# Rotary pieces of a latent attention: made at 512 queries at a time, without the second set of products, with the exchanged rows moved by GpSimd

## The reference, cut to what matters

```python
c_q, c_kv = h @ w_down_q.T, h @ w_down_kv.T          # 64 numbers a token each
q = (c_q @ w_up_q.T).reshape(b, s, H, DH)            # 16 heads of 64
k = (c_kv @ w_up_k.T).reshape(b, s, H, DH)
v = (c_kv @ w_up_v.T).reshape(b, s, H, DH)
# rope: of each head, with even rows e and odd rows o
rot = stack([e * cos - o * sin, e * sin + o * cos])
scores = einsum('bhqd,bhkd->bhqk', q, k) / sqrt(64)
out = softmax(scores) @ v
out = out @ w_out.T + x
```

## Time and profile before

| | |
|---|---|
| time of one execution, median of 3 | 2020.72 us (2020.29 to 2023.2) |
| the profiled execution: its own time | 2017.2 us |
| its span in the profile | 2015.4 us |
| PE busy | 1864.9 us (93%) |
| DVE busy | 1583.6 us (79%) |
| ACT busy | 1288.5 us (64%) |
| POOL busy | 1067.1 us (53%) |
| granted TensorE clock, mean | 0.97 |

### The profile page before, as it was taken

One profiled execution on the slowest core, in us unless ns is written; L12 is line 12 of the kernel. 1 busy time (PEld: TensorE's weight loads), 2 busy tenths in 40 slices (PEclk: granted clock), 3 DMA queues, 4 the chain that ended last, 5 costly groups with the idle time before them and its releaser, 6 DMA issues. The chain is left out here.

```text
span 2015.4 us, 36125 instructions
## 1 busy us (share of the span) xinstructions
PE 1864.9 (93%) x11446; PEld 928.7 (46%) x11446; DVE 1583.6 (79%) x2378; ACT 1288.5 (64%) x2678; POOL 1067.1 (53%) x1219
## 2 busy tenths in 40 slices
PE   5767898889868999999999999999999999999798
PEld 2553585458543444443444443444443444444446
DVE  6788865786556888887888887888888888888455
ACT  5555783578336777776777776777776777777321
POOL 0637742674226566565656655665665666566200
PEclk9898999999978999999999999999999999999799
DMA  1100302030065999988998998899899899998353
GB/s 38 66 1 6 82 3 74 6 82 3 14 263 184 331 336 343 328 321 308 324 343 325 340 333 301 318 325 346 324 334 333 310 323 335 338 333 324 127 117 74
DMA packets 201609, 454.24 MB, mean 225 GB/s; under 512 B 12064, under 2 KB 159264, under 8 KB 200256
## 3 DMA queue, kind: packets, MB, share of 16 engines
q1 hardware_dynamic: 201408, 451.76, 63.9%
HBM read 230.86 MB, written 206.83 MB: 217 GB/s over the span
## 5 line engine op out<-in xcount | busy, mean ns | idle before, releaser
L1680 ACT ACTIVATE g.probs<-g_score,g.lowest 128x1024 f32<-128x1024 f32 x514 | 567.9, 1109 | 333.3 <-DVE g.lowest L1666 333.3
L1666 DVE TENSOR_REDUCE g.lowest<-g_score 128x1 f32<-128x1024 f32 x514 | 605.7, 1220 | 186.8 <-PE g_score L1634 186.8
L1634 PE MATMUL g_score<-g.keys,g.queries 64*128 64x512 f32 x2056 | 501.6, 606 | 19.6 <-issue 11.3
L1776 DVE STREAM_TRANSPOSE g.blocks<-g.probs 128x768 f32<-128x768 f32 x512 | 467.3, 952 | 0.9
L1696 PE MATMUL g_mix_ps<-g.far,mid.y_tok 128*64 128x512 f32 x1560 | 378.1, 606 | 0.0
L1634 PEld LDWEIGHTS g_score<-g.keys,g.queries 64*128 64x128 f32 x2056 | 183.9, 188 | 249.5 <-ACT g.probs L1680 130.6
L1736 POOL TENSOR_TENSOR g.scaled<-g.scaled,g.coef 128x1024 f32<-128x1024 f32 x66 | 125.1, 1896 | 236.9 <-ACT g.scaled L1728 227.9
L1796 POOL TENSOR_TENSOR mid.y_tok<-mid.y_tok,g.waves 128x512 f32<-128x512 f32 x128 | 162.3, 1268 | 74.8 <-ACT mid.y_tok L1649 74.8
L1656 PEld LDWEIGHTS g_turned<-top.ident,g.probs 128*128 128x128 f32 x1024 | 107.8, 141 | 195.3 <-issue 195.3
L1423 POOL TENSOR_TENSOR g.queries<-mid.y_tok 64x256 f32<-64x256 f32 x256 | 185.4, 724 | 19.6
L1656 PE MATMUL g_turned<-top.ident,g.probs 128*128 128x128 f32 x1024 | 168.8, 288 | 0.0
(11 more groups left out here) (371 smaller groups left out, 2769.4 us busy)
## 6 DMA issues: line engine op xcount, KB each, us to landing
g.far<-bounce SPq DMA_DIRECT2D x257, 768.0 KB, 6.9
bounce<-g.blocks SPq DMA_DIRECT2D x256, 768.0 KB, 6.2
e.share<-shares SPq DMA_DIRECT2D x8, 1024.0 KB, 17.2
g.far<-g.near SPq DMA_DIRECT2D x7, 768.0 KB, 12.0
lt.early<-turns SPq DMA_DIRECT2D x2, 2048.0 KB, 10.2
lt.early<-la0.v SPq DMA_DIRECT2D x6, 512.0 KB, 9.3
lt.early<-la1.v SPq DMA_DIRECT2D x6, 512.0 KB, 10.2
bounce<-g.near SPq DMA_DIRECT2D x4, 768.0 KB, 18.0
```

The source lines that it names most:

```text
L1634: nc.tensor.matmul(score[:, 2 * pair + odd], queries[rows, turn, head, cols], keys[rows, turn, head, pair * CH:(pair + 1) * CH], start=Tru ...
L1666: nc.vector.tensor_reduce(lowest[:, unit, half, r:r + 1], score[:, 2 * half:2 * half + 2].rearrange("p b n -> p (b n)"), AX.X, ALU.max, ne ...
L1680: nc.scalar.activation(probs[:, r % 2, half * 2 * CH:(half + 1) * 2 * CH], score[:, 2 * half:2 * half + 2].rearrange("p b n -> p (b n)"), ...
L1776: ins = nc.vector.transpose(blocks[:, r, :, REST * half:REST * (half + 1)].rearrange("p j t c -> p t j c"), probs[:, r % 2, at:at + REST * ...
```

## The change

Three things change.

1. `pieces` makes only the plain products, of 512 tokens: two products of 512 columns in place of two times four of 256 columns. It runs once in a pass, at step 5, for the pass that follows; the first one stands ahead of the loop. ACT's `take_pieces` moves from steps 2 and 4 to step 6.
2. POOL makes the swapped part itself. `exchange` multiplies `raw` by the sine waves and writes the result 32 partitions further or back, in a new tile `exchanged`: four operations of 32 partitions and 1024 elements, each of which waits for the one ahead of it. `turn_pieces` then multiplies `raw` by the cosines (two operations of 128 x 512), and `place_pieces` subtracts: two operations of 64 x 512 for the keys and four for the queries.
3. POOL's order in a pass becomes: `gaps`, `exchange`, `turn_pieces`, keys, `add_output`, queries, `totals`, `coefs`, `gaps`, `add_output`, `totals`, `coefs`.

The diff, without the signatures that only pass `join` on:

```diff
+        exchanged = sp.sb("exchanged", [P, 2, CH])
...
         def pieces(pe, turn, at):
-            for swap in range(2):
-                for kind in range(2):
-                    ins = projected(side[:, kind, swap * QH:(swap + 1) * QH], turn, kind, swap,
-                                    slice(at * QH, (at + 1) * QH))
+            for kind in range(2):
+                ins = projected(side[:, kind], turn, kind, 0, slice(at * CH, (at + 1) * CH))
             ins.then_inc(m["piece_full"], 1)

-        def take_pieces(act, half):
-            act.wait_ge(m["parts_ready"], 2 * half + 2)
-            act.wait_ge(m["piece_full"], half + 1)
+        def take_pieces(act, n):
+            act.wait_ge(m["parts_ready"], n + 1)
+            act.wait_ge(m["piece_full"], n + 1)
             nc.scalar.activation(raw[:], side[:], ACT.Copy).then_inc(m["piece_taken"], 1)
...
+        def exchange(pool, at, n, H):
+            pool.wait_ge(m["piece_taken"], n + 1)
+            pool.wait_ge(m["gap_ready"], H + 1)
+            for k in range(4):
+                rows, other = slice(32 * k, 32 * k + 32), slice(32 * (k ^ 1), 32 * (k ^ 1) + 32)
+                if k:
+                    pool.wait_ge(m["order"], 12 * n + k)
+                nc.gpsimd.tensor_tensor(exchanged[rows].rearrange("p k (a n) -> p k a n", a=2),
+                                        raw[other].rearrange("p k (a n) -> p k a n", a=2),
+                                        waves[other, 2 * at:2 * at + 2, 1].unsqueeze(1).broadcast_to([32, 2, 2, QH]),
+                                        ALU.mult).then_inc(m["order"], 1)
+            pool.wait_ge(m["order"], 12 * n + 4)
+
+        def turn_pieces(pool, at):
+            for kind in range(2):
+                part = raw[:, kind].rearrange("p (a n) -> p a n", a=2)
+                nc.gpsimd.tensor_tensor(part, part, waves[:, 2 * at:2 * at + 2, 0], ALU.mult).then_inc(m["order"], 1)
+
+        def place_pieces(pool, turn, at, n, kind):
+            first, second = raw[:, kind], exchanged[:, kind]
+            if kind == 0:
+                for head in range(2):
+                    pool.wait_ge(m["order"], 12 * n + 6 + head)
+                    place_keys(nc.gpsimd, turn, head, at, CH, first, second, ALU.subtract).then_inc(m["order"], 1)
+                pool.wait_ge(m["order"], 12 * n + 8)
+            else:
+                for crossed in range(2):
+                    for head in range(2):
+                        place_queries(nc.gpsimd, turn, head, head ^ crossed, at, CH, first, second, ALU.subtract)\
+                            .then_inc(m["order"], 1)
+                    pool.wait_ge(m["order"], 12 * n + 10 + 2 * crossed)
+                pool.sem_inc(m["parts_ready"], 1)
...
                             last, this = (2 * j + 3) % 4, 2 * j % 4
+                            n = 4 * g + j
                             gaps(pool, last, H - 1)
+                            exchange(pool, j, n, H)
+                            turn_pieces(pool, j)
+                            if j == 0:
+                                pool.wait_ge(m["score_done"], 128 * g + 4)
+                            place_pieces(pool, 1 - turn, j, n, 0)
                             add_output(pool, (2 * j + 1) % 4, (j + 2) % NC, H)
-                            make_parts(pool, 1 - turn, 2 * j, H, 0)
+                            pool.wait_ge(m["added"], H + 2)
+                            place_pieces(pool, 1 - turn, j, n, 1)
                             totals(pool, last, H - 1)
-                            make_parts(pool, 1 - turn, 2 * j, H, 1)
-                            make_parts(pool, 1 - turn, 2 * j + 1, H + 1, 0)
                             coefs(pool, last, H - 1)
                             gaps(pool, this, H)
-                            make_parts(pool, 1 - turn, 2 * j + 1, H + 1, 1)
                             add_output(pool, (2 * j + 2) % 4, (j + 3) % NC, H + 1)
                             totals(pool, this, H)
                             coefs(pool, this, H)
...
                                     if step == 0:
                                         pe.wait_ge(m["out_taken"], H + 1)
+                                        pe.wait_ge(m["piece_taken"], 4 * g + j + 1)
                                         output(pe, mixer_now[0])
...
-                                    elif step == 1:
-                                        pe.wait_ge(m["out_taken"], H + 2)
-                                        pieces(pe, 1 - turn, 2 * j)
-                                    elif step == 3:
-                                        pe.wait_ge(m["piece_taken"], H + 1)
-                                        pieces(pe, 1 - turn, 2 * j + 1)
+                                    elif step == 5:
+                                        pe.wait_ge(m["out_taken"], H + 3)
+                                        if j < NC - 1:
+                                            pieces(pe, 1 - turn, j + 1)
+                                        else:
+                                            pieces(pe, turn, 0)
...
                                     elif step == 2:
-                                        take_pieces(act, H)
                                         falls(act, H - 1)
-                                    elif step == 4:
-                                        take_pieces(act, H + 1)
                                     elif step == 6:
+                                        take_pieces(act, 4 * g + j + 1)
                                         falls(act, H)
```

More of the change, by code:

```diff
@@ L1412, in projected, with place_keys @@
             return nc.tensor.matmul(out, w_up[rows, turn, swap * P:(swap + 1) * P], c[rows, cols], start=True, stop=True)
-        def place_keys(engine, turn, head, at, width, first, second):
+        def place_keys(engine, turn, head, at, width, first, second, join=ALU.add):
             block, inside = divmod(at * width, CH)
@@ L1418, in place_keys, with place_queries @@
             return engine.tensor_tensor(keys[block % 2 * 64:block % 2 * 64 + 64, turn, head, cols],
-                                        first[head * 64:head * 64 + 64], second[head * 64:head * 64 + 64], ALU.add)
-        def place_queries(engine, turn, head, half, at, width, first, second):
+                                        first[head * 64:head * 64 + 64], second[head * 64:head * 64 + 64], join)
+        def place_queries(engine, turn, head, half, at, width, first, second, join=ALU.add):
             return engine.tensor_tensor(queries[half * 64:half * 64 + 64, turn, head, at * width:(at + 1) * width],
-                                        first[head * 64:head * 64 + 64], second[head * 64:head * 64 + 64], ALU.add)
+                                        first[head * 64:head * 64 + 64], second[head * 64:head * 64 + 64], join)
         def load_w(sync, turn, pair):
@@ L1788, in read_blocks @@
                            bounce[4 * w + r].rearrange("(i p x) -> p i x", i=4, p=P)).then_inc(signal or landed[w], 16)
[L1790 to L1798, removed]
+        def exchange(pool, at, n, H):
[16 more added lines that the diff above has]
+            first, second = raw[:, kind], exchanged[:, kind]
             if kind == 0:
                 for head in range(2):
-                    place_keys(nc.gpsimd, turn, head, at, QH, first, second).then_inc(m["order"], 1)
-                    pool.wait_ge(m["order"], n + 2 + head)
+                    pool.wait_ge(m["order"], 12 * n + 6 + head)
+                    place_keys(nc.gpsimd, turn, head, at, CH, first, second, ALU.subtract).then_inc(m["order"], 1)
+                pool.wait_ge(m["order"], 12 * n + 8)
             else:
@@ L1805, in make_parts @@
                     for head in range(2):
-                        place_queries(nc.gpsimd, turn, head, head ^ crossed, at, QH, first, second)\
+                        place_queries(nc.gpsimd, turn, head, head ^ crossed, at, CH, first, second, ALU.subtract)\
                             .then_inc(m["order"], 1)
-                    pool.wait_ge(m["order"], n + 3 + 2 * crossed)
-            pool.sem_inc(m["parts_ready"], 1)
+                    pool.wait_ge(m["order"], 12 * n + 10 + 2 * crossed)
+                pool.sem_inc(m["parts_ready"], 1)
         MIXED_AT = (range(2, 4), range(4, 6), range(6, 8), range(0, 2))
@@ L1847, in _ @@
                 pool.sem_inc(m["added"], 1)
-                pool.sem_inc(m["parts_ready"], 2)
+                pool.sem_inc(m["parts_ready"], 1)
                 pool.sem_inc(m["combined"], 3)
@@ L1879, in _ @@
                 mix(pe, 0, range(0, 2))
+                pieces(pe, 1, 0)
                 pe.sem_inc(m["out_full"], 1)
@@ L1912, in _ @@
                                         output(pe, mixer_now[0])
-                                    elif step == 1:
+                                    elif step == 4:
                                         pe.wait_ge(m["out_taken"], H + 2)
```

(8 more changed lines are left out.)

8 lines of the change are left out of this document (5 added, 3 removed).

## The result

The changed kernel takes 2047.91 us (median of 4, 2045.26 to 2052.94), the kernel before 2020.88 in the same comparison. The ratio is 1.0135, with a 95% interval of 1.0113 to 1.0156: slower by 27 us. The forecast was 2048.

A forecast was written before the change was run, and what follows sets the result against it. PE was taken to set the pace before; after, POOL's chain would hold DVE's reciprocal. A pass of 26.65 + 12.7 = 39.35 us against 38.48 gave +27 in all, 2044 profiled, plus 3.5 for the median: 2048 us, range 2010 to 2080.

The forecast's parts named there:

- PE gains about 1 us a pass: Steps 1 and 3 lose 2.0 us, step 5 gains 0.95; PE's own pass becomes 37.4 to 37.5 us from 38.48.
- An `exchange` operation costs what 128 partitions cost: POOL's four 32 x 1024 operations were each put at 2.356 us, the price of 128 x 1024.
- The bounds 1.90 and 3.3: Lower and upper limits in us given for one `exchange` operation on POOL, around the 2.356 taken.
- POOL's chain is 26.65 us: From step 7's reciprocal, POOL's work through `totals` lets DVE's step 4 reciprocal start at 26.65 us.
- DVE stands 4.1 us at the reciprocal: At step 4, each pass: PE would bring DVE there at 22.5 us, but it waits 4.1 us for POOL's sums.
- Behind the stall DVE runs without a gap: From step 4's reciprocal to step 7's, DVE has no idle time: 12.7 us instead of 14.00, PE's step 5 work hidden.
- The sum: 26.65 + 12.7 = 39.35 us a pass against 38.48, +0.87; +24.4 over 28 ordinary passes, +27 us in all.
- The jump: At three loop jumps `gaps` starts late; such a pass takes 44.75 us against 45.10, -1.0 us for the three.
- The first pass: Products ahead of the loop and POOL's chain make the first pass late: +3.7 us.
- POOL in time: Rival: POOL's chain to `totals` stays under 25.8 us, so PE sets the pace; 1991 us at 1.90 an operation; 15%.
- The clock: Rival: PE's idle time lowers its clock, up to 1.9 us more each pass, 2108 us; 5%.
- Contention: Rival: POOL runs slower beside DVE, 3.3 us for each `exchange` operation, 3.8 us more a pass, 2166 us; 5%.

The follow-up runs named there:

- `totals` early: Changed kernel with `totals` of the last unit moved up on POOL to just behind the two cosine products, nothing left out: 1993.76 us, ratio 0.9874.
- half an operation less: Changed kernel with the first of four `exchange` operations multiplying keys only, 32 x 512 in place of 32 x 1024: 2015.17 us, ratio 0.9973.
- the kernel with the longest chain: Changed kernel with one of the `exchange` operations done twice, same result: 2190.53 us, ratio 1.0817.

## Why the prediction was right, step by step

- **PE gains about 1 us a pass.** Right. Its own pass was put at 37.4 to 37.5, and is 37.61 where nothing holds it; the group of products was put at 0.95, and doubling it makes the pass 38.48 (1290.55 to 1329.03 in that trace), 0.87 more. The gain hardly shows in PE's busy time of the changed kernel (1860.7 against 1864.9 us), where the rows of scores behind a wait are longer (2.23 us at step 6, against 1.88 with `totals` early) and count as busy; with `totals` early it is 1842.8.
- **An `exchange` operation costs what 128 partitions cost.** Right, and the step on which all hung: 2.356 taken, a median of 2.353 measured. The bounds 1.90 and 3.3 were both far off.
- **POOL's chain is 26.65 us.** Measured 26.56.
- **DVE stands 4.1 us at the reciprocal.** Measured 3.73. The term that was mis-sized is PE's part, 22.5, which is 22.75 (24.48 - 1.73): steps 1 and 3 each gave back 0.97, but step 2 grew from 4.26 to 4.37, and `row_max` of step 4 starts 1.21 us behind its scores in place of 1.11. It has no effect on the pass, since POOL's chain sets it.
- **Behind the stall DVE runs without a gap.** 12.7 taken, 12.61 measured. That the new products were hidden is shown by doubling them. PE was forecast to wait 1.9 us a pass for g.probs; the profile has 1.0 to 1.2 ahead of the scores of step 6, in 28 passes. The room that PE has in a pass is 39.17 - 37.61 = 1.56 us, and 0.35 of it lies inside those scores, which take longer than at full pace (to the next row 2.16 us in place of 1.81). POOL's rest ahead of the `coefs` of step 7 is 5.23 us, forecast 4.7.
- **The sum.** From the first to the last reciprocal of step 7 the loop takes 1231.18 us (664.21 to 1895.39) against 1208.67 (656.46 to 1865.13), 22.5 more, forecast 23.4. That match hides two misses. The 28 ordinary passes cost 19.4 us, where 24.4 were forecast: a pass is 0.69 longer and not 0.87, since both of its parts, 26.65 and 12.7, were put a tenth too long. And the three passes with a jump cost 3.1 more, where 1.0 less was forecast.
- **The jump.** This is the term that was wrong in its sign. Its new length was right, 44.75 against 44.88, 44.60 and 44.65. What it was compared with was not: 45.10 is the longest of the three in the kernel before, the others being 43.81 and 42.14 (reciprocals at 925.86 and 969.67, 1239.07 and 1284.17, 1553.58 and 1595.72). There PE's scores come back behind the jump at different speeds; the middle one of the three is in the earlier trace rows, with 3.79 us:

```profile
930.49 2.44 PE L1634 MATMUL g_score<-g.keys,g.queries 64*128 64x512 f32 x8 [3.66 <-issue]
...
1558.13 1.99 PE L1634 MATMUL g_score<-g.keys,g.queries 64*128 64x512 f32 x8 [3.59 <-issue]
```

- **The first pass** cost 4.5 instead of 3.7, once what came ahead of the loop is taken off, and there the step that failed is DVE's 12.7:

```profile
650.20 0.18 DVE L1762 RECIPROCAL g.inverse<-g.total 128x4 f32<-128x4 f32 x1 [5.34 <-POOL g.total L1758]
...
654.72 3.43 PE L1635 MATMUL g_score<-g.keys,g.queries 64*128 64x512 f32 x8 [2.65 <-ACT g.probs L1679]
...
664.21 0.17 DVE L1762 RECIPROCAL g.inverse<-g.total 128x4 f32<-128x4 f32 x1
```

664.21 - 650.20 = 14.01: in this one pass PE waited 2.65 us, and slow scores followed. With the products made twice the same wait is 1.84 us, the scores take 2.23, and the part is 12.60 (649.69 to 662.29).

- **Luck.** Loop and first pass make 27.0, as forecast, from misses of -5.0 (ordinary passes), +4.1 (jumps) and +0.8 (first pass). The mechanism and the pass of 39.17 us were forecast well; that 2047.91 meets 2048 to a tenth is luck.
- **From the profiled execution to the median.** The two profiled executions differ by 2048.08 - 2017.2 = 30.9 us, not by 27. 3.25 of it lie ahead of the loop, in code that was not changed: its first scores start at 615.74 instead of 612.49. In the profiles of the ten edits they start anywhere from 613.06 to 618.15, so this looks like scatter between executions, which is not shown further. The forecast had 2044 for the profiled execution and added 3.5 for the median; the execution took 2048.08, and the median lies 0.2 below it. These two misses cancel as well.
- **Rivals.** POOL in time: the break-even was put at a chain of 25.8; half an operation less gave 25.47 and 2015, just under the kernel before, as the break-even says. The clock: at step 6 it fell only in the first of this kernel's 32 passes (in the others PE waits 1.2 us at most there), but real, at 64 us for 2.4 us more of chain. Contention: not seen, 2332 to 2370 ns over 128 operations. These times decide it; the section of the Trainium skill that the prediction goes by ("GPSIMD Engine Reference", Specifications) names a second case beside VectorE's two SBUF inputs, its 2-port modes, which the prediction did not weigh.

## What to carry to other kernels

Taking work off the busiest engine pays only as far as the next handover lets it: find the instruction that waits for the engine that gets the work (here a reciprocal of 0.17 us), count what now stands ahead of what it waits for, and compare with when the busiest engine would reach it. Where such a chain is too long, move the small thing that others wait for ahead of the bulk: two operations of 0.2 us in another place turned +27 us into -26. And a stall on TensorE has a second price, its clock, that came here at times behind 2.34 us of idle time.

## What the runs showed of the hardware that had not been expected

- A GpSimd TENSOR_TENSOR takes the same for 32, 64 or 128 partitions (32 x 1024: 2.353 us; 128 x 1024: 2.356; 64 x 512: 1.263; 128 x 512: 1.268), and one starts 0.08 us after the other, wait or no wait.
- More work can make a kernel faster: 0.86 us of repeated products in each pass took 41 us off the kernel with the longest chain (2190.53 to 2149.86), since they kept TensorE's idle time at 2.6 us instead of 3.5.
- Slow scores came in 14 of 30 passes with waits of 2.34 to 2.71 us, in 16 of 29 at 2.56 to 2.76, and in all 32 at 3.42 to 5.06; behind waits of 1.0 to 1.2 us in none of 28. But 3.59 us of idle time at a loop's jump had full-speed scores behind it.
